# Layers 1 and 3 of a four-layer graph network: the last column of nine gather blocks fetched by SyncE, one row per transfer

## What is computed

```python
# layer 1, graph attention with 8 heads of 64
h = (x @ W).reshape(n, H, DIM)
a_src = jnp.einsum('nhc,hc->nh', h, att_src)
a_dst = jnp.einsum('nhc,hc->nh', h, att_dst)
logits = jax.nn.leaky_relu(a_src[src] + a_dst[dst], negative_slope=NEG_SLOPE)
e = jnp.exp(logits - seg_max[dst])
alpha = e / denom[dst]
msg = h[src] * alpha[:, :, None]
out = jax.ops.segment_sum(msg, dst, num_segments=n)
...
# layer 3, propagation weighted by the cosine of the two nodes of an edge
Wh = h @ W + b
Wr = Wh[row]
Wc = Wh[col]
sim = dot / jnp.maximum(nr * nc, EPS)
prop_pos = jax.ops.segment_sum((base * sim_pos)[:, None] * Wc, row, num_segments=n_nodes)
prop_neg = jax.ops.segment_sum((base * sim_neg)[:, None] * Wc, row, num_segments=n_nodes)
```

## Time and profile before

| | |
|---|---|
| time, median of 3 runs | 3941.34 us (3940.43 to 3942.44) |
| profiled execution, span from the first to the last instruction | 3095.7 us |
| median less span | 845.6 us |
| GpSimd busy | 2190.4 us, 71% of the span |
| VectorE busy | 1326.6 us, 43% |
| PE busy | 610.1 us, 20% |
| ScalarE busy | 481.9 us, 16% |
| transfers | 248.04 MB, 80 GB/s over the span |

### The profile page before, as it was taken

How to read it: one execution, slowest core, us unless ns; L and a number is a source line. 1 busy time by engine, 2 the same in 40 slices (tenths; PEclk the granted TensorE clock), 3 DMA queues, 4 the chain that set the end, 5 groups by cost and what they waited for, 6 DMA issues and landing times.

```text
span 3095.7 us, 14532 instructions
## 1 busy us (share of the span) xinstructions
PE 610.1 (20%) x3300; PEld 466.1 (15%) x3301; DVE 1326.6 (43%) x1981; ACT 481.9 (16%) x447; POOL 2190.4 (71%) x2299
## 2 busy tenths in 40 slices
PE   5521130001410000001888860000000400000001
PEld 5411110001300000001676640000000300000001
DVE  8888885202310000008466643233244615353455
ACT  2200006211100000000000022223223212111220
POOL 0177777777777777777777777777777377777774
PEclk8665565555555555555899875555555555555555
DMA  9311114212344755645355424323232123223231
GB/s 325 112 25 14 14 27 100 64 34 63 66 52 53 67 57 60 65 52 65 106 135 155 111 50 74 109 91 128 91 109 92 45 56 85 78 72 91 72 90 52
DMA packets 192274, 248.04 MB, mean 80 GB/s; under 512 B 135507, under 2 KB 146381, under 8 KB 184662
## 3 DMA queue, kind: packets, MB, share of 16 engines
q0 software_dynamic: 74048, 114.24, 19.1%
q1 hardware_dynamic: 60102, 103.67, 10.0%
q10 hardware_dynamic: 58064, 29.51, 7.9%
HBM read 154.17 MB, written 93.09 MB: 80 GB/s over the span
## 4 chain that ended last, share of the span: by engine, by line
POOL 55%; issue 19%; DVE 2%; ACT 0%; DMA 0%; DVEq 0%; POOLq 0%; ACTq 0%
POOL l1g_rows L831 13%; POOL l2g_rows L831 13%; POOL l3g_rows L831 12%; POOL ep_rows L1370 11%; POOL ep_rows L1351 2%; POOL l2t_res L2457 1%; POOL l3t_res L2866 1%; POOL l0f_res L1008 1%; DVE l3g_banks L2813 0%; DVE l3g_banks L2837 0%; ACT l3g_banks L2771 0%; DVE l3g_banks L2834 0%; DVE l3g_dot L2820 0%; DVEq L2819 0%; POOL ep_rows L1379 0%
## 5 line engine op out<-in xcount | busy, mean ns | idle before, releaser
L878 POOL DMA_INDIRECT l0g_rows<-in_rec_s,ents x440 | 427.4, 971 | 137.6 <-issue 133.9
L831 POOL DMA_INDIRECT l2g_rows<-tab,ep_rows x440 | 416.8, 947 | 134.2 <-issue 134.2
L831 POOL DMA_INDIRECT l1g_rows<-tab,srct x440 | 416.8, 947 | 134.2 <-issue 134.2
L831 POOL DMA_INDIRECT l3g_rows<-tab,others x440 | 416.1, 946 | 134.2 <-issue 134.2
L1370 POOL DMA_INDIRECT ep_rows<-recp,entd x352 | 338.7, 962 | 107.3 <-issue 107.3
L1572 DVE TENSOR_TENSOR l1s_A<-l1s_bank,l1s_mk 110x512 f32<-110x512 f32 x8 | 5.2, 686 | 528.4 <-PE l1s_bank L1534 528.4
L1831 PE MATMUL l1a_pa<-l1a_g,l1a_wt 128*128 x1296 | 169.6, 291 | 0.0
L1831 PEld LDWEIGHTS l1a_pa<-l1a_g,l1a_wt 128*128 128x128 f32 x1296 | 158.9, 202 | 23.8 <-issue 23.8
L2811 DVE COPY l3g_banks<-l3g_q 128x65 f32<-128x65 f32 x12 | 2.7, 229 | 306.8 <-ACT l3g_banks L2771 306.4
L2397 DVE COPY l2g_mix<-l2g_q 128x64 f32<-128x64 f32 x11 | 2.5, 228 | 306.9 <-ACT l2g_mix L2358 306.9
L1534 PE MATMUL l1s_bank<-ident,atp 128*110 128x128 f32 x64 | 10.9, 347 | 539.7 <-ACT atp L1473 530.6
(11 more groups left out here) (582 smaller groups left out, 2330.2 us busy)
## 6 DMA issues: line engine op xcount, KB each, us to landing
l1a_g<-g SPq DMA_DIRECT2D x54, 390.0 KB
recp<-ep_rows ACTq DMA_DIRECT2D x11, 1320.0 KB, 5.9
g<-l1g_rows ACTq DMA_DIRECT2D x10, 1430.0 KB, 22.7
sums<-l0s_sums SPq DMA_DIRECT2D x10, 1408.0 KB, 5.1
sums<-l2o_sums SPq DMA_DIRECT2D x9, 1408.0 KB, 4.9
sums<-l3o_sums SPq DMA_DIRECT2D x9, 1408.0 KB, 5.3
rowsd<-ep_rows POOLq DMA_DIRECT2D x8, 1452.0 KB, 5.9
ep_rows<-rowsd SPq DMA_DIRECT2D x8, 1452.0 KB, 6.6
```

What stands on the lines that cost most here:

```text
L831: nc.gpsimd.indirect_dma_start(out=ring.rows[:, s, j, :], out_offset=None, in_=table, in_offset=bass.IndirectOffsetOnAxis(ap=index(b, s, j ...
L878: nc.gpsimd.indirect_dma_start(out=rows[:, j, :], out_offset=None, in_=K.a["rec_s"], in_offset=bass.IndirectOffsetOnAxis(ap=K.by_src.ent[: ...
```

## The change

GpSimd leaves out column 43 (`SINGLE`) of blocks 0 to 8 (`SINGLES`) in layers 1 and 3. SyncE fetches that column instead, with one transfer for each of its 128 rows, whose address comes from a register. 32 row numbers (`AT_ONCE`) are loaded into registers by one tensor load. Whoever uses a block now waits for two semaphores, the 43 columns of GpSimd and the slot's `single`, which counts 128 transfers of 16.

```diff
+SINGLE = TB - 1
+SINGLES = NBLK - 1
+AT_ONCE = 32
...
+def fetch_rows(K, sp, rows, table, numbers, k, most, landed):
+    for p in range(0, P, AT_ONCE):
+        begins = values(K.nc, numbers[0:1, k * P + p:k * P + p + AT_ONCE], mybir.EngineType.SP, most)
+        for i in range(AT_ONCE):
+            sp.dma_start(rows[p + i:p + i + 1, :], table(begins[i])).then_inc(landed, 16)
...
         for j in range(TB):
+            if b < singles and j == SINGLE:
+                continue
             landed = ring.gathered[s]
...
# layer1_gather, ScalarE (now written out for every block)
-                    act.wait_ge(ring.gathered[s], ring.base[s] + (it + 1) * TB * 16)
+                    act.wait_ge(ring.gathered[s], ring.base[s] + ((it + 1) * TB - singles(it, s)) * 16)
+                    act.wait_ge(K.l1.single[s], singles(it, s) * P * 16)
...
+def layer1_singles(K):
+        @block.sync
+        def _(sp):
+            sp.wait_ge(K.l1.numbered, 1)
+            for b in range(SINGLES):
+                s, it = b % RING, b // RING
+                if it:
+                    sp.wait_ge(kept[s], it)
+                    sp.wait_ge(stored[s], it * 16)
+                fetch_rows(K, sp, ring.rows[:, s, SINGLE, :], lambda n: K.tab1[bass.ds(n, 1), :], K.sources, b, NP - 1, K.l1.single[s])
...
# layer1_items, SyncE and VectorE
+                sp.dma_start(K.sources[:, :].rearrange("o (b p) -> o b p", p=P),
+                             K.pairs[0:SINGLES * TB * P].rearrange("(b t p) -> t b p", t=TB, p=P)[SINGLE:SINGLE + 1]).then_inc(K.l1.listed, 16)
                 sp.wait_ge(far, 1)
...
+                dve.wait_ge(K.l1.listed, 16)
+                v.tensor_scalar(K.sources[:, :], K.sources[:, :], 0xFFF, None, ALU.bitwise_and).then_inc(K.l1.numbered, 1)
...
# layer2_tail, SyncE, ahead of the stores of the table
+                sp.wait_ge(offset, 2)
+                    sp.dma_start(K.numbersd.rearrange("k p -> p k"), by_src.other[:, SINGLE:SINGLES * TB:TB]).then_inc(listed, 16)
+                sp.wait_ge(listed, 32)
+                sp.dma_start(K.numbers[:, :], K.numbersd.rearrange("k p -> (k p)").unsqueeze(0)).then_inc(listed, 16)
...
# layer3_gather, SyncE
+                def fetch(b):
+                    s, it = b % RING, b // RING
+                    if it:
+                        sp.wait_ge(freed[s], it)
+                    fetch_rows(K, sp, ring.rows[:, s, SINGLE, :], lambda n: entries[bass.ds(n, R3)].unsqueeze(0), K.numbers, b,
+                               NP * R3N - R3, single[s])
+
+                sp.wait_ge(*K.tab3_stored)
+                sp.wait_ge(K.l1.listed, 48)
+                for b in range(RING):
+                    fetch(b)
                 for i, (b, c0, n, landed, count) in enumerate(parts):
+                    if i and RING + i - 1 < SINGLES:
+                        fetch(RING + i - 1)
                     sp.wait_ge(packed, i + 1)
...
# layer3_gather, ScalarE (VectorE likewise)
                     act.wait_ge(landed, count)
+                    if i < SINGLES:
+                        act.wait_ge(single[b % RING], (b // RING + 1) * P * 16)
```

More of the change, by code:

```diff
@@ L155, in build @@
         K.tab3 = dram("tab3", (NP * R3N // R3, R3))
+        K.numbersd = dram("numbersd", (SINGLES, P), I32)
         K.tab3n = K.tab3.rearrange("a b -> (a b)").rearrange("(n r) -> n r", r=R3N)
@@ L170, in build @@
                     K.l1 = SourceRows(rows)
-                    layer1_gather(K)
+                    with nc.sbuf_tensor("sources", [1, SINGLES * P], I32) as K.sources:
+                        layer1_gather(K)
+                        layer1_items(K)
+                        layer1_singles(K)
                     layer1_softmax(K)
@@ L179, in build @@
                     layer1_tail(K, T)
-            with nc.sbuf_tensor("wh", [P, NT, R3], F32) as K.wh:
+            with nc.sbuf_tensor("wh", [P, NT, R3], F32) as K.wh, \
+                    nc.sbuf_tensor("numbers", [1, SINGLES * P], I32) as K.numbers:
                 with Phase(K, "l2o") as ph:
@@ L816, in block_cols, with gather_blocks @@
 def block_cols(it, s, size=RING):
-    return bass.ds((it * size + s) * TB, TB)
-def gather_blocks(nc, pool, ring, table, index, ready, last=None, axis=0):
+    return slice((it * size + s) * TB, (it * size + s + 1) * TB)
+def fetch_rows(K, sp, rows, table, numbers, k, most, landed):
[3 more added lines that the diff above has]
+            sp.dma_start(rows[p + i:p + i + 1, :], table(begins[i])).then_inc(landed, 16)
+def gather_blocks(nc, pool, ring, table, index, ready, last=None, axis=0, singles=0):
     for b in range(NBLK):
@@ L834, in gather_blocks, with pieces @@
             ).then_inc(landed, 16)
-def pieces(ring, last):
-    whole = [(b, 0, TB, ring.gathered[b % RING], ring.base[b % RING] + (b // RING + 1) * TB * 16) for b in range(NBLK - 1)]
+def pieces(ring, last, singles=0):
+    whole = [(b, 0, TB, ring.gathered[b % RING], ring.base[b % RING] + (b // RING + 1) * (TB - (b < singles)) * 16) for b in range(NBLK - 1)]
     return whole + [(NBLK - 1, c, n, sem, base + n * 16) for (c, n), (sem, base) in zip(LAST, last)]
@@ L1446, in __init__ @@
         self.stored = [ph.sem(f"stored{s}") for s in range(RING)]
+        self.single = [ph.sem(f"single{s}") for s in range(RING)]
+        self.listed, self.numbered = ph.sems("listed", "numbered")
 def layer1_gather(K):
@@ L1464, in _, with singles @@
             store_edges(K, nc, pool, slice(RING * TB, (RING + 1) * TB), 0, TB * 16)
-            gather_blocks(nc, pool, ring, K.tab1, lambda b, s, j: K.srct[:, b * TB + j:b * TB + j + 1], ready)
+            gather_blocks(nc, pool, ring, K.tab1, lambda b, s, j: K.srct[:, b * TB + j:b * TB + j + 1], ready,
+                          singles=SINGLES)
         @block.scalar
         def _(act):
-            def body(it, first):
+            def singles(it, s):
+                return min(it + 1, len(range(s, SINGLES, RING)))
+            for it in range(NBLK // RING):
                 for s in range(RING):
-                    act.wait_ge(ring.gathered[s], ring.base[s] + (it + 1) * TB * 16)
+                    act.wait_ge(ring.gathered[s], ring.base[s] + ((it + 1) * TB - singles(it, s)) * 16)
+                    act.wait_ge(K.l1.single[s], singles(it, s) * P * 16)
                     act.dma_start(K.g1[:, block_cols(it, s), :], ring.rows[:, s, :, 0:D + 1]).then_inc(stored[s], 16)
                     nc.scalar.copy(K.atp[:, block_cols(it, s), :], ring.rows[:, s, :, D + 1:D + 17]).then_inc(kept[s], 1)
-            rounds(act, body)
-    layer1_items(K)
+def layer1_singles(K):
+    nc = K.nc
+    ring, kept, stored = K.l1.ring, K.l1.kept, K.l1.stored
+    with Step(nc, meet=False) as block:
+        @block.sync
[7 more added lines that the diff above has]
+                fetch_rows(K, sp, ring.rows[:, s, SINGLE, :], lambda n: K.tab1[bass.ds(n, 1), :], K.sources, b, NP - 1, K.l1.single[s])
 def edge_order(K):
@@ L2425, in layer2_tail @@
     nc = K.nc
-    by = K.by_dst
+    by, by_src = K.by_dst, K.by_src
     with Phase(K, "l2t") as ph:
@@ L2447, in layer2_tail @@
         added, summed, tabled, stored = ph.sems("added", "summed", "tabled", "stored")
+        offset, listed = K.l1.numbered, K.l1.listed
         K.tab3_stored = (stored, NG * 16)
@@ L2462, in _ @@
                 rows = lambda t: t.rearrange("(w p) r -> p w r", p=P)
+                sp.wait_ge(offset, 2)
+                with nc.allow_non_contiguous_dma(reason="one column of numbers for each of nine blocks, once"):
+                    sp.dma_start(K.numbersd.rearrange("k p -> p k"), by_src.other[:, SINGLE:SINGLES * TB:TB]).then_inc(listed, 16)
+                sp.wait_ge(listed, 32)
+                sp.dma_start(K.numbers[:, :], K.numbersd.rearrange("k p -> (k p)").unsqueeze(0)).then_inc(listed, 16)
                 for g, (w, n) in enumerate(GROUPS):
@@ L2617, in _ @@
                 v.tensor_tensor(other[:, :], whole[:, 0:J], whole[:, J:2 * J], ALU.add)
-                v.drain()
+                v.drain().then_inc(offset, 1)
                 wide = lambda c, ws, n: c[:, ws].unsqueeze(2).to_broadcast([P, n, D])
@@ L2727, in layer3_gather @@
         last = [ph.gather_sem(f"last{i}") for i in range(len(LAST))]
-        freed = [ph.sem(f"freed{s}") for s in range(RING)]
+        freed, single = ([ph.sem(f"{n}{s}") for s in range(RING)] for n in ("freed", "single"))
         out = K.sums3.rearrange("(p j) d -> p j d", p=P)
-        parts = pieces(ring, last)
+        parts = pieces(ring, last, SINGLES)
         def cut(t, f, n):
@@ L2746, in ready @@
                         pool.wait_ge(freed[s], it)
-                gather_blocks(nc, pool, ring, K.tab3, lambda b, s, j: K.by_src.other[:, b * TB + j:b * TB + j + 1], ready, last, axis=1)
+                gather_blocks(nc, pool, ring, K.tab3, lambda b, s, j: K.by_src.other[:, b * TB + j:b * TB + j + 1], ready, last, axis=1, singles=SINGLES)
             @block.sync
             def _(sp):
```

(7 more changed lines are left out.)

## The result

The changed kernel takes **4822.97 us** (median of 4 runs, 4821.06 to 4824.12) against 3941.36 for the kernel before: 1.2237 times as long, interval 1.2219 to 1.2254, or 882 us more. I had forecast 4117, with a range up to 4285: the sign was right, the size was not.

A forecast was written before the change was run, and what follows sets the result against it. GpSimd's gathers were taken to bound the kernel, with SyncE's slower columns becoming the pace: 3941.3 us plus 100 (layer 1) and 76 (layer 3) gave 4117 us, range 3965 to 4285.

The forecast's parts named there:

- What bounds the kernel: Layers 1 and 3: GpSimd's back-to-back gathers set the pace, 1.252 us a column, 55.1 us a block of 44.
- 845.6 us above the span; no row divides that, and I let it stand.: Whole kernel: timed median 3941.34 us against the trace's 3095.7 us span; the difference was kept unchanged in the forecast.
- What SyncE's new work costs: SyncE, per column: 128 rows of 433 ns, 55.4 us, plus four 32-register loads, 7.7 us with gaps; 63.1 us.
- the signs of "right": One-row transfers about 0.26 us, 0.43 apart; loads 1.9 us; GpSimd waiting from the third block; layer end times; issue gaps after stores.
- F against 53.8 us: Both gathers: SyncE's 63.1 us per column exceeds GpSimd's 53.8 us for 43 columns, so SyncE sets the pace.
- The stores' hold on SyncE, 35 us: Layer 1: ScalarE's stores delay SyncE's issue by 5 us each, seven stores, 35 us.
- my +100: Layer 1: SyncE's column pace and the stores move the gather's end from 1394.4 to 1494.2 us, +100 us.
- my +76: Layer 3: SyncE's nine columns make block 8 land at 3055.9 instead of 2980.13 us, +76 us.
- The cover of the new preparation steps: VectorE's extra layer 1 operation hides under the gather; layer 3's two new transfers in layer2_tail cost nothing.
- A row costs as much as 128 rows: Rival, both layers: a transfer takes 332 ns, a row 0.509 us; +178 and +164, 4283 us; chance 0.10.
- stores shut SyncE out: Rival, layer 1: each store stops SyncE's issue for all its 20 us; +207, total 4224 us; chance 0.16.
- Faster: Rival, both layers: SyncE's column fits under GpSimd's 53.8 us, each gaining nine columns, 11.3 us; 3919 us; chance 0.10.

The follow-up runs named there:

- e1: The kernel before the change, run and traced once more with no edit: 3941.76 us, with a span of 3939.9 us.
- e2: The changed kernel with SyncE fetching its nine columns in layer 1 alone, layer 3 as in the kernel before: 4362.40 us.
- e3: The changed kernel with SyncE fetching its nine columns in layer 3 alone, layer 1 as in the kernel before: 4409.59 us.
- after: The changed kernel itself, SyncE fetching nine columns row by row in layers 1 and 3, against the kernel before: 4822.97 us.
- e7: The changed kernel with each SyncE column fetched in four transfers of 32 fixed rows instead of 128 of one row: 3921.12 us.
- e4: The changed kernel with the 128 transfers per column fetching fixed rows, without register loads and register instructions: 4317.66 us.
- e5: The changed kernel with all columns back on GpSimd and SyncE running long-satisfied waits beside layer 1's gather: 3947.09 us.
- e6: The changed kernel with GpSimd gathering 22 instead of 43 columns per block from the third block on, layers 1 and 3: 4453.80 us.

## Why the prediction was wrong, point by point

- **What bounds the kernel: right for its trace, and not for the timed runs.** GpSimd never waits in the gathers, in e1 either (its rows above). But I read stretches beside GpSimd at a pace that the timed runs do not have.
- **The step that failed: "845.6 us above the span; no row divides that, and I let it stand."** I carried the difference over as a constant. By e1 it is what the hold costs: against the earlier trace GpSimd waits some 630 us longer for work that the other engines could not do beside its gathers (most of it in the first two rows below, waits that the trace of before doesn't have), and its gathers and edge rows take some 210 us longer. This grows with the instructions that a change puts beside the gathers. It should have been a sign that no price taken from that trace holds beside a gather.

```profile
POOL l2g_first L2283 <- DMA tab<-l1f_tab: 346.6, 1, 346.6
POOL l0f_res L1008 <- DVEq L1027: 177.6, 1, 177.6
...
POOL l3t_res L2866 <- DMA sums<-l3o_sums: 30.5, 1, 30.5
```

- **What SyncE's new work costs: right by itself.** A row is 0.41 us (forecast 0.433), a load of 32 registers 2.12 us (1.9), a column in the clear 128 x 0.406 + 4 x 2.12 = 60.5 us (F = 63.1). The Trainium skill ("DMA: Bandwidth & Descriptors", section Latency and other measured facts) has about 600 ns as the floor of a tensor load; no run shows such a floor: a load of one register took 268 ns. So the signs of "right" that I had named for these prices were nearly met, as was GpSimd's wait before each block, and a row of 0.406 us just touches a sign of "wrong" (below 0.41): the signs tried the prices, not the overlap.
- **F against 53.8 us: the comparison failed.** It took the slower of two engines that run side by side. With the hold they nearly add up: 53.5 us of gather, in which 29 to 35 rows pass, and 52.8 us for the others, per block. Both layers' excess rests on this: layer 1 is +421 (e2) for my +100, layer 3 +468 (e3) for my +76.
- **The stores' hold on SyncE, 35 us: wrong.** ScalarE issued a store at 1404.88 in after, and in the 15.3 us that follow SyncE fetched 31 rows, 0.43 us each when the one load among them is taken off. Behind each of the eight stores that a column follows it is 34 or 35 rows in 20 us. The queues from 1405.5 to 1424.0 us, the store's first and then SyncE's (packets, MB, and the packets' times added up as a share of the engines' time):

```profile
q10 hardware_dynamic: 5648, 1.46, 113.7%
q1 hardware_dynamic: 51, 0.01, 1.4%
```

The rule of the Trainium skill that I weighed there ("DMA: Bandwidth & Descriptors", section Queues, rings and completion order), taking turns packet by packet, agrees with this: SyncE's packets pass during the store. When its rows landed, the trace does not show.
- **Layer 1, where the rest goes.** From the rows of e1 and after GpSimd's gather grows from 586.0 to 996.3 us (+410.3). Its wait for layer 1's result grows from 346.6 to 369.8 (+23.2), its edge rows shrink from 494.0 to 478.3 (-15.7). That is +418. The edge rows in e1 (its waits stand above), then those of after with its waits for layer 1's result and for the last sums:

```profile
L1370 POOL DMA_INDIRECT ep_rows<-recp,entd x352 | 340.4, 967 | 153.6 <-issue 153.6
```

```profile
L1389 POOL DMA_INDIRECT ep_rows<-recp,entd x352 | 336.6, 956 | 141.7 <-issue 141.7
```

```profile
POOL l2g_first L2327 <- DMA tab<-l1f_tab: 369.8, 1, 369.8
...
POOL l3t_res L2935 <- DMA sums<-l3o_sums: 102.0, 1, 102.0
```

- **Layer 3.** The gather grows from 590.3 to 981.0 us (+390.7); GpSimd's wait for the last sums, ahead of the final lookup, from 30.5 to 102.0 (+71.5), since the work behind block 8 begins late, as I had it. That is +462; with layer 1's +418 it makes 880 of the 882.2 by which the spans differ. The chain of after there, in order of time, answers the ScalarE row:

```profile
4706.32 5.50 ACT l3g_banks L2838
```

- **The cover of the new preparation steps: right.** SyncE's column is all that the chain shows. GpSimd waits before each block from the third on, as forecast.
- **Rivals.** None had this mechanism. "A row costs as much as 128 rows" came nearest in time, 4283, from a row of 0.51 us that in the clear is 0.41; "stores shut SyncE out", 4224, has a cause that isn't there. "Faster" had its condition, a column under GpSimd's 53.8 us, met by no real fetch; e7 puts its gain at 18 us, near my 22.

## What to carry to other kernels

Where the span of a trace and the timed runs differ by a fifth, first get a trace of an execution that agrees with them; a difference carried along as a constant can be the very thing that a change multiplies. Work moved off a busy engine isn't side by side with it just because it has a queue of its own: count the instructions that the move adds beside the gathers, 3456 and 36 loads here per layer in place of 9 on GpSimd. This holds for executions like the timed ones; the change has not been run in one without the hold, so what it costs there is open. None of these runs beats the kernel before with real row numbers, and the most that the idea could give is 18 us in 3940.

## What the runs showed of the hardware

- In the timed executions, while GpSimd issues indirect transfers, the other engines' instructions pass, once the hold has set in, at 1.0 to 1.4 us each if one engine has many: 2.9 to 3.1 us for a row of three instructions (after), 1.28 to 1.38 for a row of one (e4), 1.39 for a bare wait (e5). For the compute engines together it was one in 0.57 us beside the edge rows of e1. The steps are mostly multiples of 0.7 us. The hold sets in 4.3 to 9.3 us after a gather begins and lasts 6.9 to 7.4 us beyond its end (after), as if something fills and empties; what, no run shows. GpSimd itself is slowed by little, 1.25 to 1.4 us a column against 1.25 without the hold.
- It isn't the load on the transfer engines: SyncE's rows went on at 0.43 us beside ScalarE's store. That GpSimd's gathers are the condition is shown by e6, where the held time shrank with them, and by e1, where the other engines run freely once they are over. Whether other work of GpSimd's would do the same was not tried.
- What makes the limit stays open. The same program ran without it once, in the trace of before, so it isn't in the program alone. The Trainium skill ("NOTIFIC — Programmer's Manual", section When the ring fills) says that the queue of an engine's records can be set to make the engine block until there is room; no run here shows whether records have a part in this. The landings that only the trace of before has (e1) make it a rival to be tried first.
- A load of 32 registers on SyncE takes 2.12 us (median, after) where one takes 0.27.
